# PSUM banks in one pool, norms on ScalarE, and attention heads turned in squares of 32 on VectorE, in a five-phase cross-attention kernel

## The reference

```python
# L0: cross-attention with rotary positions, plus the input
q, k = rope(x @ Wq.T + bq), rope(ctx @ Wk.T);  v = ctx @ Wv.T + bv
x = softmax(q k^T / sqrt(8)) v @ Wo.T + bo + x
# L1: adaptive norms (shift, scale, gate from ctx[:, 0:2]); x is cut into halves of 128 rows
x0, x1 = halves(x);  each += gate * mha(mod(ln(half)))           # self-attention of each half
xm, ym = mod(ln(x0)), mod(ln(x1))                                # each half attends to the other
x = x + gate * concat(attend(xm, ym), attend(ym, xm))
x = x + gate * mlp(mod(ln(x)))                                   # 128 -> 512 -> 128, gelu
# L2: cross-attention to ctx, plus x, then layer norm with gamma and beta
# L3: layer norm, cross-attention to ctx with weights quantised to -1, 0, 1, plus x
```

## Time and profile before

| | |
|---|---|
| time, median of 3 runs | 326.67 us (325.97 to 326.98) |
| time of the profiled execution | 323.99 us |
| its span, first to last instruction | 322.2 us |
| busiest engines | PE 282.4 us, DVE 248.7 us, ACT 229.4 us, POOL 183.9 us |
| mean TensorE clock granted | 0.970 of full speed |

### The profile page before, as it was taken

The page is one execution under the profiler, slowest core; times in us unless marked ns, Lnnn a source line. Parts: engine busy times, 40 slices in busy tenths (PEclk is TensorE's granted clock), DMA queues, the critical chain, the costliest instruction groups (busy, mean ns, idle before and its releaser), DMA issues.

```text
span 322.2 us, 8824 instructions
## 1 busy us (share of the span) xinstructions
PE 282.4 (88%) x3152; PEld 159.6 (50%) x3152; DVE 248.7 (77%) x549; ACT 229.4 (71%) x486; POOL 183.9 (57%) x269
## 2 busy tenths in 40 slices
PE   4448999889998888899889899989989999899994
PEld 3324534434444556567567566555453545444432
DVE  5446899999776598879666785988988889888812
ACT  2121256778888776697787869988877878798881
POOL 7783410685696886747485836682667876720000
PEclk9995789999999999999999999999999999999998
DMA  4589254803131332232222112212121313030001
GB/s 125 147 216 253 74 139 118 256 18 77 35 92 29 77 85 52 67 101 75 65 69 60 42 38 69 65 35 54 50 68 38 80 32 90 22 83 21 17 4 33
DMA packets 40747, 24.73 MB, mean 77 GB/s; under 512 B 4856, under 2 KB 39552, under 8 KB 40576
## 3 DMA queue, kind: packets, MB, share of 16 engines
q1 hardware_dynamic: 39024, 22.70, 26.9%
q0 software_dynamic: 384, 1.05, 1.4%
q10 hardware_dynamic: 1296, 0.42, 0.5%
HBM read 7.56 MB, written 0.54 MB: 25 GB/s over the span
## 4 chain that ended last, share of the span: by engine, by line
PE 49%; DVE 23%; issue 8%; ACT 6%; POOL 6%; DMA 4%; SPq 2%; POOLq 0%; ACTq 0%; DVEq 0%
PE ps_small L664 13%; PE ps_heads L664 13%; DVE neg_max L1034 9%; PE ps_score L664 8%; PE ps_max L664 8%; DVE normed L466 3%; DMA rope_wide<-in_rope,pos_row 3%; POOL normed L466 2%; PE ps_small L838 2%; SPq L436 2%; DVE stats L997 2%; ACT probs L886 2%; PE ps_small L852 2%; POOL rstd L635 2%; PE ps_small L842 1%
## 5 line engine op out<-in xcount | busy, mean ns | idle before, releaser
L1034 DVE TENSOR_REDUCE neg_max<-ps_max 128x2 f32<-128x512 f32 (+1 forms) x256 | 160.7, 681 | 20.5 <-PE ps_max L664 19.5
L886 ACT ACTIVATE probs<-ps_score 128x512 f32<-128x512 f32 x256 | 141.2, 600 | 21.6 <-PE ps_score L664 19.4
L664 PE MATMUL ps_score<-q_stack,k_stack 64*128 64x256 bf16 (+1 forms) x640 | 81.8, 252 | 0.7 <-DMA q_stack<-max_rows 0.2
L664 PE MATMUL ps_max<-k_stack,q_stack 62*128 62x256 bf16 (+1 forms) x640 | 77.9, 257 | 2.3 <-DVE neg_max L1034 1.5
L664 PE MATMUL ps_heads<-probs,v_cols 128*32 128x256 f32 (+1 forms) x1280 | 77.2, 344 | 0.2 <-ACT probs L886 0.2
L664 PEld LDWEIGHTS ps_max<-k_stack,q_stack 62*128 62x128 bf16 x640 | 34.8, 95 | 32.6 <-DVE neg_max L1034 15.6
L664 PEld LDWEIGHTS ps_score<-q_stack,k_stack 64*128 64x128 bf16 x640 | 34.9, 94 | 31.6 <-ACT probs L886 19.2
L664 PEld LDWEIGHTS ps_heads<-probs,v_cols 128*32 128x32 f32 x1280 | 29.7, 108 | 23.3 <-issue 13.8
L416 POOL TENSOR_TENSOR split_r<-q_f,k_parts 128x256 f32<-128x256 f32 x20 | 13.4, 671 | 45.1 <-issue 35.5
L664 PE MATMUL ps_small<-src_t,w 128*128 128x256 f32 x96 | 32.0, 441 | 1.3 <-ACT k_parts L927 0.4
L635 POOL TENSOR_TENSOR rstd<-var_eps,minus_half 128x2 f32<-128x2 f32 x20 | 14.4, 718 | 25.7 <-DVE var_eps L1002 25.7
(11 more groups left out here) (110 smaller groups left out, 395.2 us busy)
## 6 DMA issues: line engine op xcount, KB each, us to landing
k_stack<-k_parts SPq DMA_DIRECT2D x120, 64.0 KB, 2.1
q_stack<-q_parts SPq DMA_DIRECT2D x114, 64.0 KB, 2.1
w<-in_w SPq DMA_DIRECT2D x3, 512.0 KB, 4.1
gates<-gate_row SPq DMA_DIRECT2D x1, 1536.0 KB, 6.7
rows<-in_rows SPq DMA_DIRECT2D x1, 704.0 KB, 7.2
w<-in_w SPq DMA_DIRECT2D x1, 576.0 KB
q_stack<-max_rows SPq DMA_DIRECT2D x36, 8.0 KB
ctx_t<-in_ctx_t SPq DMA_DIRECT2D x4, 128.0 KB, 2.9
```

What stands on the lines that cost most here:

```text
L664: return nc.tensor.matmul(out, lhs_t, rhs, start=start, stop=stop, **k)
L886: nc.scalar.activation(probs[:, n % PROB_BUFS, :], ps_score[n % SCORE_BUFS][:, :], ACT.Exp, scale=SCALE).then_inc(exped, 1)
L1034: nc.vector.tensor_reduce(dst, src, AX.X, ALU.max, negate=True).then_inc(max_taken, 1)
```

## The change

- **Heads.** After the last `value` of a unit VectorE turns `ps_heads` itself, in squares of 32 by 32, into `heads_raw`; takes the reciprocal and multiplies as before, but now out of SBUF; and turns `heads` once more in squares into `heads_q`. ScalarE adds the bias from there. ScalarE's copy and the steps `unstack` and `heads_t` on TensorE are gone; `headrow` orders the rows of the output weights for it on the host.
- **Norms.** ScalarE makes `normed` in all phases, as scale times x plus shift; POOL works out the shift (minus mean times rstd) from `less_mean`, a new small instruction of VectorE. ScalarE's queue waits for `rstd_ready` there.
- **Banks.** The seven banks other than `ps_heads` are one pool. `BANK_OF` gives the bank of each writer in order, and a writer waits until the last user of its bank is done with it.
- **Rotary tables.** The gathers fetch 128 bytes a row into `rope_rows`, and ScalarE spreads each value eight times into `rope_wide` (`expand`).
- **Start.** `rows`, `x` and all weights but the first two groups are loaded from ScalarE's queue; `rows`, `x` and `ada` stand ahead of `expand` there. One third of the clearing of `q_stack` goes from VectorE to POOL, and POOL's first `clear_v` behind the first gather. In the new order the third unit's rotary turn (`rope`, 2) stands behind the first nine `max` steps; before, it stood ahead of all.
- **Stacking.** `split` makes the second part first and signals it, and `place_parts` sends each part when it is there. The numbers of DMAs stay.
- **Order.** `ORDER` is a new string throughout.

```diff
-SMALL_BUFS, MAX_BUFS, SCORE_BUFS = 2, 3, 2
+BANKS = 7
...
-          ("max_t", 1), ("max_t", 4),
-          ("norm", 0), ("norm", 1), ("norm", 2))
+          ("max_t", 1), ("max_t", 4))
...
-ROPE_COLS = 2 * D
+ROPE_COLS = 4 * DH
+SQUARE = 32
...
-        "O": [("small", k, u) for u in units for k in ("unstack", "heads_t", "out_proj")],
+        "O": [s for u in units for s in (("turn", u, 0), ("bias", u, 0), ("small", "out_proj", u))],
...
+    writers = [st for st in steps if st[0] in ("max", "score", "small")]
+    bank = {st: int(b) for st, b in zip(writers, "".join(BANK_OF), strict=True)}
...
-                    if n >= MAX_BUFS:
-                        pe.wait_ge(max_taken, n - MAX_BUFS + 1)
-                    out = ps_max[n % MAX_BUFS]
+                    if occupant[st]:
+                        pe.wait_ge(*emptied(occupant[st]))
+                    out = ps[bank[st]]
...
-                    nc.gpsimd.tensor_tensor(rstd[:, :], var_eps[:, :], minus_half[:, :], ALU.pow).then_inc(rstd_ready, 1)
+                    link(nc.gpsimd.tensor_tensor(rstd[:, :], var_eps[:, :], minus_half[:, :], ALU.pow))
+                    nc.gpsimd.tensor_tensor(shift[:, :], less_mean[:, :], rstd[:, :], ALU.mult).then_inc(rstd_ready, 1)
...
-                    elif kind == "unstack":
-                        pe.wait_ge(heads_copied, u + 1)
-                        for qt in range(NT):
-                            for g in range(2):
-                                last = nc.tensor.transpose(out[:, (qt * 2 + g) * P:(qt * 2 + g + 1) * P],
-                                                           heads_raw[:, g * T + qt * P:g * T + (qt + 1) * P], ident)
-                    elif kind == "heads_t":
-                        for qt in range(NT):
-                            last = nc.tensor.transpose(out[:, qt * P:(qt + 1) * P], heads[:, qt, :], ident)
...
+                elif st[0] == "expand":
+                    b = st[1]
+                    act.wait_ge(gathered[b], NT * 16)
+                    nc.scalar.activation(rope_wide[...], rope_rows[...] broadcast, ACT.Copy).then_inc(rope_expanded, 1)
+                elif st[0] == "apply":
...
+                    act.wait_ge(rstd_ready, no("norm", u, st[2]) + 1)
...
+                    for qt in range(NT):
+                        last = nc.scalar.activation(normed[:, qt, :], src[:, qt, :], ACT.Identity,
+                                                    bias=shift[:, qt:qt + 1], scale=rstd[:, qt:qt + 1])
+                    last.then_inc(applied, 1)
+                elif st[0] == "bias":
+                    u = st[1]
+                    act.wait_ge(heads_turned, u + 1)
...
+                    nc.scalar.activation(heads_t[:, :], heads_q[:, :], ACT.Identity, bias=V(f"bv{PHASE[u]}")
+                                         ).then_inc(heads_biased, 1)
...
+                nc.vector.tensor_scalar(less_mean[:, :], mean_var[:, :, 0], -1.0, None, ALU.mult)
...
+                elif st[0] == "turn":
+                    u = st[1]
+                    dve.wait_ge(valued, VALUES * (u + 1))
+                    nc.vector.transpose(heads_raw[:, :], ps_heads[:, :]).then_inc(heads_copied, 1)
+                    dve.wait_ge(heads_copied, u + 1)
+                    src = heads_raw[:, :].rearrange("p (m e) -> p m e", e=2 * DH)
+                    link(nc.vector.reciprocal(inv_sum[:, :], src[:, :, DH]))
+                    link(nc.vector.tensor_tensor(heads[:, :, :, :].rearrange("p g q (i e) -> p (g q i) e", e=DH),
+                                                 src[:, :, 0:DH], inv_sum[:, :].unsqueeze(2).broadcast_to([P, 2 * H, DH]),
+                                                 ALU.mult))
+                    dve.wait_ge(heads_biased, u)
+                    nc.vector.transpose(heads_q[:, :].rearrange("p (q e) -> p q e", e=SQUARE),
+                                        heads[:, :, :, :].rearrange("p g q e -> p q g e")).then_inc(heads_turned, 1)
```

More of the change, by code:

```diff
@@ L163, in make_schedule @@
         "s": [("score", u, c) for u in units for c in range(n_chunks(u))],
-        "R": [("rope", b, 0) for b in range(B)],
+        "R": [s for b in range(B) for s in (("expand", b, 0), ("rope", b, 0))],
         "G": [("small", "mod", 0), ("small", "gate", 0), ("gate_store", 0, 0), ("gate_spread", 0, 0), ("small", "gamma", 0)],
@@ L183, in build @@
         seen[st[0]] = order[st] + 1
+    writers = [st for st in steps if st[0] in ("max", "score", "small")]
+    bank = {st: int(b) for st, b in zip(writers, "".join(BANK_OF), strict=True)}
+    small_bank = [bank[st] for st in writers if st[0] == "small"]
+    occupant = {}
+    last_on = {}
+    for st in writers:
+        occupant[st] = last_on.get(bank[st])
+        last_on[bank[st]] = st
     def no(*step):
@@ L289, in build @@
         small_ready = sem("small_ready")
-        small_used = [sem(f"small_used{i}") for i in range(SMALL_BUFS)]
+        small_used = [sem(f"small_used{i}") for i in range(BANKS)]
         max_scored = sem("max_scored")
@@ L337, in used, with emptied @@
         def used(n):
-            return small_used[n % SMALL_BUFS], n // SMALL_BUFS + 1
+            return small_used[small_bank[n]], small_bank[:n + 1].count(small_bank[n])
+        def emptied(st):
+            if st[0] == "small":
+                return used(no(*st))
+            return (max_taken if st[0] == "max" else exped), no(*st) + 1
         def operands(kind, u):
@@ L849, in _ @@
                     elif kind == "norm_t":
-                        pe.wait_ge(norm_ready, earlier(u, 0, 1, 2, 3) + 1)
+                        pe.wait_ge(applied, no("apply", u, int(phase == 3)) + 1)
                         for qt in range(NT):
@@ L914, in _ @@
                     n = no(*st)
[L915 removed]
+                    ps_small = ps[bank[st]]
                     phase, b = UNIT[u]
@@ L1193, in constants @@
     return {"const": np.eye(P, dtype=np.float32),
-            "rope": np.broadcast_to(table[:, :, None, :, None], (MAX_POS, 2, 2, DH, PAIRS)).reshape(MAX_POS, ROPE_COLS)}
+            "rope": np.repeat(table[:, :, None, :], 2, axis=2).reshape(MAX_POS, ROPE_COLS)}
 def kernel(**inputs):
```

250 lines of the change are left out of this document (123 added, 127 removed).

## The result

The changed kernel takes 309.42 us (median of 4 runs, 308.69 to 310.57) against 326.32 us of the kernel before (324.41 to 326.98): a ratio of 0.9495 [0.9442, 0.9548], 5% faster. Forecast were 308 us in a range from 298 to 320, and a gain of 5.7%. The profiled execution took 309.96 us with a span of 308.2 us; the one before took 323.99 us with 322.2 us.

The account below looks back on a forecast made before the run. VectorE and TensorE were taken to share the bound (0.58). The span, 322.2 - 10.3 - 5.7 - 2.0 - 0.8 = 303.4 us, plus 1.8 and 2.7 us of offsets gave 307.9, so 308 us, range 298 to 320.

Parts of the forecast that it names:

- The new instructions: VectorE's head work: turns +1.10 us a unit, reciprocal -0.13, multiplication +0.17, together +1.14 us a unit.
- the rival of squares at double cost: VectorE's turns cost double, giving DVE 22 us more: 315 us in all; chance 0.12.
- The term of +0.17 us: Heads multiplication, both operands now from SBUF: +0.17 us a unit, between 0 and 0.49; 0.20 by POOL's busy time.
- The outer stretches: Outside 100 to 220 us: PE 150.0 plus DVE 156.7 us at a joint 183% take 167.6 us, -5.7.
- PE's 11.5 us are mostly given back to DVE: Outer stretches: PE loses 11.5 us of work, DVE's rises from 146.0 to 156.7 us; only -5.7 us results.
- The middle: Phases 1 and 2, 100 to 220 us: PE's 99.3 us at 90.6% busy take 109.7 us, -10.3.
- Slower, ScalarE waits for rstd: At 20 norms ScalarE waits up to 1.44 us for rstd and shift, 29 us in all: 337 us; chance 0.10.
- ScalarE holds the middle: ScalarE can't pass 82.5% busy in the middle, so its 99.6 us take 120.7 us: 319 us; chance 0.12.
- The shared banks give more: PE reaches 95% in the middle and the outer sum 188%, 9.6 us more gained: 298 us; chance 0.08.
- Start and end: Start: first maximum earlier, -2 us taken. End: shorter chain from last copy to last addition, -0.8 us.
- The bound on the start: Start: loads ahead of expand run beside the first gather and may cost up to +4 us, so perhaps no gain.
- I give it no term: Banks and order: later bank refills help hold the assumed busy shares, but nothing was added to the sum.

Follow-up runs that it names:

- a_robin: Changed kernel with its seven pooled banks taken in rotation instead of by the handwritten list: 313.55 us, ratio 0.9635 to the kernel before.
- a_pe_turns: Changed kernel with six dead 128x128 turns a unit on TensorE ahead of the output projection, results overwritten: 314.17 us, ratio 0.9688 to the kernel before.
- a_turn_twice: Changed kernel with each unit's first VectorE turn made twice, the spare one ahead of the real one: 324.01 us, ratio 0.9924 to the kernel before.
- a_turn_apart: Changed kernel with a spare 128x512 VectorE turn a unit behind the second turn, where nobody waits: 317.71 us, ratio 0.9748 to the kernel before.
- a_act_more: Changed kernel with ScalarE's bias pass made three times a unit instead of once: 322.62 us, ratio 0.9859 to the kernel before.
- a_heads_back: a_robin with the heads turned as before (ScalarE's copy, six turns on TensorE): 336.32 us, ratio 1.0279 to the kernel before.
- a_norms_back: Changed kernel with norms back on VectorE (phases 0 to 2) and POOL (phase 3), without less_mean and shift: 320.89 us, ratio 0.9869 to the kernel before.
- b_norms: Kernel before with only the norms moved to ScalarE, with less_mean and shift: 340.66 us, ratio 1.0452.

## Why the prediction was right, step by step

**The size.** 309.4 us against 308 is nearer than the steps deserve, and in part luck. The sum gave a span of 303.4 us and the profile has 308.2: 4.8 us too short. Part of that was made good by the offset of 2.7 us between the profiled run and the median of before: this time the profiled run lies 0.5 us above its median, not below.

**The new instructions.** Turns and multiplication, which answer to the earlier trace rows:

```profile
L1084 DVE STREAM_TRANSPOSE heads_raw<-ps_heads 128x512 f32<-128x512 f32 x20 | 14.1, 707 | 4.5 <-PE ps_heads L682 4.3
L1093 DVE STREAM_TRANSPOSE heads_q<-heads 128x256 f32<-128x256 f32 x20 | 8.9, 445 | 0.7
L1088 DVE TENSOR_TENSOR heads<-heads_raw,inv_sum 128x256 f32<-128x256 f32 x20 | 8.8, 439 | 0.7
L1087 DVE RECIPROCAL inv_sum<-heads_raw 128x32 f32<-128x32 f32 x20 | 7.1, 353 | 0.7
```

The turns cost 1.15 us a unit where the nearest rows gave 1.10: one stream of columns, as the argument had it, and the rival of squares at double cost is gone. The prediction's estimate from the Trainium skill (Vector Engine (DVE) Microarchitecture Reference, The reshape front-end and per-opcode configuration, and VectorE: DVE Perf Modes, The three transpose paths), 0.71 and 0.44 us, agrees to about 1%. Two terms were mis-sized and cancel in part. The reciprocal costs 0.353 us out of SBUF as it did out of PSUM, not 0.22: +2.7 us over 20 units. The multiplication met POOL hardly at all:

```profile
L1088 DVE TENSOR_TENSOR heads<-heads_raw,inv_sum x20: 424/425/621, 59.5 to 302.7; 128x256 f32<-128x256 f32 x20
```

The term of +0.17 us measured +0.015, or -3.1 us over 20 units. The Trainium skill's rule (SBUF — State Buffer, Who interferes with whom) isn't refuted by it, since single ones took up to 0.621 us, and `q_f` of the same form up to 0.634 (median 0.425, mean 0.468); but to price it by POOL's busy share was wrong for this instruction. DVE's total came to 256.0 us (forecast 261), PE's to 259.9 (261).

**The outer stretches.** That PE and DVE are what is nearly full there held; that their shares add to a fixed sum did not. I took 183% for the two together. From unit 0 to unit 3 PE has 92.0% and DVE 90.6%, 182.6% together; in the late stretch 92.0 and 88.2%, 180.2% (the profile was to show DVE at 90% or more). Four variants are near this in the late stretch (a_robin 179.3, a_pe_turns 181.1, a_turn_twice 179.4, a_turn_apart 180.3%), but others aren't: the kernel before has 176.7%, a_act_more 175.0, a_heads_back 163.2. From 209 to 273 us DVE hardly pauses:

```profile
209.00:241.00 32.00, 29.61 (x325) 14.55 (x324) 31.15 (x77) 27.68 (x64) 15.79 (x26) 1.00 0.23 58
241.00:273.00 32.00, 29.88 (x317) 14.47 (x316) 31.31 (x78) 28.17 (x63) 18.03 (x29) 1.00 0.23 58
```

That is 97 and 98%, and 190 and 191% with PE's, above the 183%: in these 64 us DVE is the one that is full. The dead work agrees, each figure within about 1 us. In the late stretch 5.1 us more of DVE's busy time cost 4.3 us (a_turn_apart) and 4.0 us more of PE's cost 2.0 (a_pe_turns), where a common sum of 183% would charge 0.55 us for each us of either; and ScalarE's, which the step left out, cost 4.1 us for 5.7 (a_act_more). "PE's 11.5 us are mostly given back to DVE" was right, and more so than the sum had it: in the late stretch all of it was given back (-0.1), and the 3.5 us won lie before unit 3.

**The middle.** The number nearly held (-10.3 against -9.1), the reason in part. The prediction let PE's busy time alone set the time, at 90.6%, 1.10 us for each us of work, and took ScalarE and VectorE as having slack. At full clock dead work on PE costs about that, 4.0 us for 3.4. But ScalarE's costs nearly as much (3.9 for 4.4) and VectorE's about half (2.2 for 4.2), each give or take 1 us, though neither is busy for more than 83% in `after`. So there is no slack that can be filled for nothing, and the bound isn't PE's alone. a_norms_back shows a second thing, the hand-overs of a unit: PE's work unchanged, nobody full, and 5.4 us longer in four units, of which DVE's added work explains some 1.8 by the estimate above. a_heads_back (middle +8.8) doesn't decide, since it has 9.8 us more of PE's busy time and the hand-overs too. Undoing the norms or the heads costs 7.8 and 8.8 us in the middle, together more than the 9.1 us won, so the gain can't be divided between the parts.

That the number came so near is again in part luck: in the two units with a fallen clock `after` is 3.1 us longer than a_pe_turns, which has more work. And 7.5 of the 9.1 us lie between units 9 and 11, where PE's busy time fell by 6.5 us; whether the new order only moved steps out of these two units wasn't tried.

From the first instruction that empties `ps_heads` to the addition the kernel after needs 3.7 us in the median over units 3 to 11, the one before 5.1 (the spread is wide, 3.4 to 8.0 and 4.2 to 6.4); counted from the end of the last value it is 4.3 and 5.2. That this shorter path gives part of the 9.1 us is argued, not shown: the runs that make it longer (a_pe_turns, a_act_more) put work on an engine at the same time.

**The rivals.** "Slower, ScalarE waits for rstd" is refuted by the idle time in front of its norms:

```profile
L924 ACT ACTIVATE normed<-x,shift,rstd 128x128 f32<-128x128 f32 x24 | 10.7, 508 | 0.0
L924 ACT ACTIVATE normed<-gated,shift,rstd 128x128 f32<-128x128 f32 x16 | 7.2, 521 | 0.0
```

In 20 norms it never waited: the order puts `apply` late enough. In the old order it did, 11.4 us in b_norms, so the rival's mechanism is real, and the kernel after avoids it, by its order as I read it. "ScalarE holds the middle" didn't come true either: 82.0% of the middle, not 90.8, and from unit 0 to unit 3 `after` has 87.6%, above the 82.5% that the rival took as its limit. Work added to it isn't free, though, as the middle shows. Its total is 229.2 us where I summed 238, though a norm costs 0.51 us and not 0.458. The sum missed that busy time counts overlap once: 256 exponentials, 620 ns each in the mean instead of 600, are busy for 134.8 us instead of 141.2. The Trainium skill (ScalarE: Activation LUTs, Rules for kernel authors) would keep multiply-and-add on VectorE; in the new order a_norms_back says the opposite, 12 us dearer with the norms off ScalarE, and in the old order b_norms agrees with the page, 4.5% slower with the norms on it. "The shared banks give more" was a rival for 298 us; the runs turn it round: the banks give nothing by themselves and are what the rest stands on.

**Start and end.** The bound on the start held: the loads slow the first gather, 2.78 to 5.90 us, and the first maximum gains 1.0 us instead of 2. At the end the chain of 4.16 us became 3.95: the copy and PE's turns are gone, but the last projection takes 1.20 us instead of 0.70. TensorE did nothing for 2.79 us ahead of it, through DVE's turns, and over these 1.20 us the granted clock was 0.50, where it had been 1.00 over the 0.70:

```profile
301.53 0.73 DVE heads_raw L1084
303.60 0.52 ACT heads_t L932
304.25 1.20 PE ps L682 x4
```

Over the whole last stretch it is 0.63, in the fourth row of the stretches after; before it was 0.83. I priced the removal of work from TensorE and not what its idleness costs it.

**What the prediction left out.** "I give it no term" for banks and order. Each part alone, in the old order, made the kernel slower or changed nothing (+8.0, +4.5, -0.4%), and the new order without the pool is 16% slower. How much of the gain is the order's own couldn't be tried apart from the parts, since the order's letters fit only one set of steps. It stays open, as does what the rotary tables, the start and the stacking gave, which were never undone alone, and the part of a_act_more's 12 us that its profile doesn't show.

## What to carry to other kernels

With in-order queues and banks handed round by a written order, a busy share of 82 to 88% doesn't say that an engine has slack: dead work on each of three engines made the middle longer. When you test with dead work, cut the trace by units and compare only those with the same granted clock; over the whole middle, the clock here turned 4.0 us into 0.9 in one run, and parted two runs by 6.7 us that are equal at full clock. And a part of a change that is tried alone in an order made for another kernel measures the order, not the part: here two parts alone cost 8 and 4.5%, the third gave 0.4%, and the whole gained 5%.

## What the runs showed of the hardware

- A turn in squares of 32 on VectorE, f32: 128x512 out of PSUM 707 ns (694 to 717), 128x256 within SBUF 445 ns, near the 679 ns of the maximum's reduction over 512 columns and the 425 ns of the multiplication over 256. The reciprocal of 128x32 takes 353 ns out of either memory.
- At a lower granted clock the same matmuls take longer. In `after`, PE is busy for 6.05 of 8 us and then runs at 0.57:

```profile
121.00:129.00 8.00, 6.05 (x108) 3.85 (x107) 6.80 (x18) 7.11 (x18) 4.57 (x8) 1.00 0.33 84
129.00:137.00 8.00, 7.52 (x107) 5.89 (x111) 5.63 (x15) 3.96 (x9) 4.48 (x8) 0.57 0.35 91
```

  A mean of 0.57 is most of those 8 us at the lower of the two levels, 1.2 instead of 2.4 GHz. The middle's 1190 matmuls were busy for 79.37 us here, for 76.88 in a_turn_apart at 1.00 and for 82.45 in a_turn_twice at 0.91.
- Pauses alone don't foretell a fall. In a_norms_back PE is busy for 5.35 of 8 us, less than above, and the clock stays in the next 8:

```profile
105.00:113.00 8.00, 5.35 (x91) 3.69 (x86) 6.91 (x17) 4.21 (x11) 4.56 (x7) 1.00 0.27 71
113.00:121.00 8.00, 6.85 (x134) 5.26 (x135) 7.03 (x19) 6.14 (x15) 4.55 (x7) 1.00 0.31 78
```

  The middle of a_pe_turns, with its dead turns, had no fall, but neither had those of a_robin, a_turn_apart and a_act_more, which put nothing on TensorE. That work taken from TensorE costs it clock isn't shown: the four runs of `after` have 0.963 in the mean, 45 of the kernel before 0.967.
- An indirect gather whose rows became eight times shorter still went from 2.78 to 5.90 us once three loads were issued beside it.
